# A graph kernel's two edge sorts: one more 512-column product in each half step of the position loop

## The reference, cut to what matters

```python
edge_index = jnp.stack([src, dst])
h = jnp.maximum(_layernorm(x, axis=-1), 0.0)
x = x + _L0_gnn_ref(h, ..., edge_index, edge_type_64, 0)      # attention over relations, 3 hops
...
x = x + _L1_gnn_ref(h, edge_index, ...)                       # graph attention, 3 layers
...
x = x + _L2_gnn_ref(h, src, dst, ...)                         # graph convolution
...
x = x + _L3_gnn_ref(h, ..., src, dst, edge_type_474)          # composed attention
```

## Time and profile before

| | |
|---|---|
| median of 3 runs | 10832.68 us (10826.94 to 10835.59) |
| profiled execution, its own time | 10814.64 us |
| its span, first to last instruction | 10812.8 us |
| mean granted clock of PE | 0.785 |
| position loop, first sort | 272.6 to 745.5 us |
| position loop, second sort | 1012 to 1487 us |

### The profile page before, as it was taken

One profiled execution on the slowest core, in us unless ns is written; L12 is line 12 of the kernel. 1 busy time (PEld: TensorE's weight loads), 2 busy tenths in 40 slices (PEclk: granted clock), 3 DMA queues, 4 the chain that ended last, 5 costly groups with the idle time before them and its releaser, 6 DMA issues. The chain is left out here.

```text
span 10812.8 us, 222859 instructions
## 1 busy us (share of the span) xinstructions
PE 6848.0 (63%) x64938; PEld 5402.2 (50%) x64939; DVE 8324.0 (77%) x22674; ACT 6175.0 (57%) x11492; POOL 6853.0 (63%) x5770
## 2 busy tenths in 40 slices
PE   3984952236666566656666477777777768466665
PEld 2973952235554455545555344444544534366665
DVE  9779778857777677767777699899989970477776
ACT  4224222236666566646666499899979960155554
POOL 0777731057776777767777488878868610466665
PEclk8555556568887788877888799999999989777777
DMA  0111114322222222222222211111111126322212
GB/s 22 57 37 28 60 33 143 129 61 53 53 53 48 49 53 53 53 46 52 53 53 53 38 43 49 50 38 49 46 41 49 49 72 250 74 48 47 46 45 44
DMA packets 415976, 627.20 MB, mean 58 GB/s; under 512 B 273479, under 2 KB 327073, under 8 KB 392169
## 3 DMA queue, kind: packets, MB, share of 16 engines
q0 software_dynamic: 192432, 385.10, 16.3%
q1 hardware_dynamic: 156048, 155.60, 4.6%
q10 hardware_dynamic: 67401, 85.32, 2.2%
HBM read 525.80 MB, written 101.39 MB: 58 GB/s over the span
## 5 line engine op out<-in xcount | busy, mean ns | idle before, releaser
L895 POOL DMA_INDIRECT l_land<-table,l_words x3744 | 3580.1, 956 | 1338.0 <-issue 1153.7
L1674 POOL DMA_INDIRECT ell<-gat_stage_pay,gat_stage_at x816 | 1899.5, 2328 | 248.7 <-issue 248.7
L1365 PE MATMUL left_product_ps<-k_w,messageT 128*128 128x128 f32 x5616 | 1036.5, 341 | 531.6 <-ACT messageT L1400 531.6
L1365 PEld LDWEIGHTS left_product_ps<-k_w,messageT 128*128 128x128 f32 x5616 | 873.4, 237 | 736.4 <-ACT messageT L1400 736.4
L1723 PE MATMUL gat_ps<-gat_probT,h 128*32 128x128 f32 x15000 | 823.7, 292 | 436.2 <-ACT gat_probT L1774 290.3
L2234 PE MATMUL rel_ps<-relation_parts,hot 128*128 128x128 bf16 x11328 | 821.0, 247 | 414.8 <-DVE hot L2333 414.6
L244 POOL DMA_INDIRECT ell<-pay,position x816 | 841.6, 1031 | 290.8 <-issue 281.6
L1359 PE MATMUL left_turned_ps<-ident,message 128*128 128x128 f32 x2808 | 557.7, 333 | 728.2 <-DVE message L1491 728.2
L2234 PEld LDWEIGHTS rel_ps<-relation_parts,hot 128*128 128x128 bf16 x11328 | 800.7, 113 | 436.2 <-DVE hot L2333 436.2
L1416 ACT ACTIVATE weighed<-kept,l_prob 128x128 f32 x2784 | 889.1, 391 | 59.1 <-ACT l_prob L961 59.1
L1714 PE MATMUL gat_ps<-ident,gat_logit 128*128 128x128 f32 x5625 | 824.5, 285 | 44.4 <-ACT gat_logit L1767 43.3
(11 more groups left out here) (332 smaller groups left out, 16142.2 us busy)
## 6 DMA issues: line engine op xcount, KB each, us to landing
gcn_edges<-counts SPq DMA_DIRECT2D x50, 1600.0 KB, 7.4
l_land<-table,l_words POOLq DMA_INDIRECT x3744
rows<-low_dram SPq DMA_DIRECT2D x34, 1536.0 KB
counts<-pair_turned_sb ACTq DMA_DIRECT2D x12, 3200.0 KB, 9.4
logs<-pair_logs ACTq DMA_DIRECT2D x12, 3200.0 KB, 18.2
ell<-pay,position POOLq DMA_INDIRECT x816
ell<-gat_stage_pay,gat_stage_at POOLq DMA_INDIRECT x816
l_words<-ell SPq DMA_DIRECT2D x476, 8.0 KB
```

Source lines behind the costliest of these rows:

```text
L895: pool.indirect_dma_start(self.land[:, p, s, :], None, table[:, :], bass.IndirectOffsetOnAxis(ap=self.words[:, p, s, 0:1], axis=0)).then_i ...
L1365: mm = pe.matmul(right_ps[:, k * H + j, :], messageT[:, k, j, :], k_w[:, :], start=True, stop=True)
L1674: pool.indirect_dma_start(c.ells[1][:, :], bass.IndirectOffsetOnAxis(ap=stage_at[n % 2][:, t:t + 1], axis=0), stage_pay[n % 2][:, t, :], N ...
```

## The change

Each half step of the position loop gets one more product between `match(n + 1)` and `look(n)`. Its stationary operand is `ident_b`, its moving operand the 512 columns of `earlier`, its output the whole bank of `most_ps`, which is widened from 128 to 512 columns for it. No one reads the result, and it signals no one and waits for nothing. The earlier uses of `most_ps` name their 128 columns.

```diff
-    most_ps = pb("most_ps", [P, P])
+    most_ps = pb("most_ps", [P, H * P])
...
-                pe.transpose(most_ps[0:NB, :], block_most[:, :], c.ident[:, :]).then_inc(most_turned, 1)
+                pe.transpose(most_ps[0:NB, 0:P], block_most[:, :], c.ident[:, :]).then_inc(most_turned, 1)
...
+                def keep_warm():
+                    pe.matmul(most_ps[:, :], ident_b[:, :], earlier[:, :, :].rearrange("p s e -> p (s e)"),
+                              start=True, stop=True)
...
                         if not (last and r == HF - 1):
                             match(n + 1, r + 1)
+                        keep_warm()
                         look(n, r, k * CT + r * H)
...
-                step(V.tensor_reduce(most_of[:, :], most_ps[0:NB, :], AX.X, ALU.max))
+                step(V.tensor_reduce(most_of[:, :], most_ps[0:NB, 0:P], AX.X, ALU.max))
```

## The result

The changed kernel takes 10940.49 us (median of 4 runs, 10937.15 to 10946.35), the kernel before 10830.04 us (10826.94 to 10835.59): ratio 1.0101, 95% interval 1.0088 to 1.0114. It is 110 us slower; 109 were forecast, as 10943 us.

A forecast was written before the change was run, and what follows sets the result against it. PE was taken to bound the two position loops at clock 0.50. 342 products x 0.32 us = 109 us, added to 10832.7, gave 10942, rounded up to 10943 us; range 10922 to 10992 us.

The forecast's parts named there:

- What paces the loop: Two position loops: PE sets the pace, except DVE at chunk ends; each microsecond more in a loop lengthens the kernel equally.
- The net price: Product before line 295's loads: 0.427 us raw, less 0.10 us of the first load it hides, taken as 0.32 us.
- covers the 0.10 us: Before line 295: the new product hides the 0.10 us of the first load that stick out behind line 284.
- How many count: Both loops: 342 of 408 products cost time; at chunk ends PE's wait for DVE, 1.46 us, falls to 0.7 us.
- The clock: Position loops: PE's granted clock stays at 0.50, since a denser stretch of relation attention did not hold it up.
- The rival of a risen clock: Position loops: clock rises and stays, DVE paces at 1.99 us a half step; 73 us less, 10760 us; chance 0.07.
- A longer loop only gives them more room: POOL's first-sort DMAs make their last start 61 us before the second loop ends, so lengthening the loop delays nothing there.

The follow-up runs named there:

- e1: Changed kernel with the added product moved before match(n + 1); 13708.98 us against 13586.41 for the kernel before, on a slow chip.
- e2: Changed kernel with the added product cut from 512 to 128 columns; 13641.09 us against 13586.41 for the kernel before, on a slow chip.
- e5: Changed kernel with the added product cut from 512 to 256 columns; 10858.07 us against 10825.11 for the kernel before.
- e3: Changed kernel with two added products of 512 columns a half step; 13802.44 us against 13586.41 for the kernel before, on a slow chip.
- e4: Changed kernel with four added products of 512 columns a half step; 14074.71 us against 13586.41 for the kernel before, on a slow chip.
- e6: Changed kernel with 68 more products ahead of each position loop; 10925.49 us in one run, beside 10825.11 for the kernel before.
- e7: e6 with three products a half step and six more in each chunk's second half step; 10845.66 us against 10825.11 for the kernel before.
- e10: Kernel before with only 48 of POOL's 816 indirect DMAs of line 244; 12741.68 us against 13582.89 with all, on a slow chip.

## Why the prediction was right

- *What paces the loop.* Right: all of the loss is in the two loops, and all of it passes to the end.
- *The net price.* Right at 0.32 us (2.49 - 2.17), and by its reason: one load runs ahead under the product in front of it. Moving the product costs 0.10 us more (`e1`), and 128 and 256 columns cost the same 0.107 us (`e2`, `e5`). The price is the longer of the product and the 0.213 us load, less the 0.106 us that stuck out: 0.107, 0.107 and 0.32 us for 128, 256 and 512 columns. What I had written, that a product "covers the 0.10 us", holds only for one longer than the load; `e2`'s expectation fell by that. (The prediction's 0.427 - 0.10 is 0.327; with 0.106 for what sticks out it is the 0.32 that was used.) The Trainium skill, "TensorE: Matmul & The Clock Gate", section "The mechanism", has loads overlap running products only of other row groups. These runs do not agree with it: the loads here use the whole array, and the half step grew by 0.32 us and not by the product's 0.43.
- *How many count.* Right: 0.68 us of idle time at a chunk's end (forecast 0.7), chunks of 31.0 us, 109.4 us in the loops for 342 x 0.32 = 109.
- *The clock.* Right that it stays at 0.50, in both loops and also with two and four products a half step (`e3`, `e4`). The reason given, a comparison with one stretch of relation attention, is only argued: no run here tells what the clock goes by. Whether one product a half step would hold a clock that is up was not shown either (`e6`).
- *The rival of a risen clock.* Its condition did not come about, and its price was wrong. The 10760 us took DVE's pace, 1.99 us, from a sum of durations, where DVE kept up with 1.78 us in `e7`; and they overlooked POOL's DMAs of line 233: the loops fell by 155 us in `e7`, and the time rose by 20. "A longer loop only gives them more room" was right for the forecast and was the very sentence to turn round for the rival.

## What to carry to other kernels

A product added in front of a weight load costs, in this loop at the low clock, the longer of its columns and the load behind it, less what of the load stuck out before; read this from the start of the next load. PE's busy share does not tell what clock it will get: loops that are fully busy run at either level. Before pricing a faster loop, look for the stream that would end last without it, down to its last instruction; here POOL's lay only 30 us ahead of the loop's end, and with one DMA of 78.6 us it ate 155 us of gain.

## What the runs showed that was not expected

- The same loop body runs at both clocks: three products a half step at 0.50 in 3.35 us, at 1.00 in 1.78 us, PE busy without a gap each time. Four a half step stayed at 0.50 for 771 us.
- On the slow chips the first loop all but stops while POOL issues its DMAs. The kernel before with few places (`e10`), 50 us with line 244 running and 50 us without, on chip 2:

```profile
330.00:380.00 50.00, 5.22 (x32) 4.50 (x32) 3.29 (x10) 1.24 (x2) 38.10 (x40) 0.50 0.02 1
420.00:470.00 50.00, 47.11 (x348) 46.58 (x348) 35.26 (x121) 13.34 (x22) 0.00 (x0) 0.50 0.18 63
```

A chunk takes 84.5 us with them and 27.8 us without; on chip 11 27.8 us with them. What in the chips makes the difference was not found.
- One indirect DMA instruction of POOL took 78.6 us (`e7`), 56.1 us (the changed kernel) and 56.9 us (`e6`) during DVE's counting, where the median is 0.96 us; the two profiles of the kernel before and that of `e5` show none above 16.2 us. What brings it about is open.
